# A tuned attention and NF4 feed-forward kernel on one core: the block sums of x for the second token unit made by GpSimd in place of VectorE

## The chip, the cores and the metric

The kernel runs on one core of one Trainium2 chip. The metric is device time in microseconds (us), from one execution to the next of the same program; less is better. A core has five engines that run their own instruction streams and meet only through semaphores: TensorE (PE in the profile) multiplies, VectorE (DVE), ScalarE (ACT) and GpSimd (POOL) work elementwise, and SyncE (SP) issues the DMAs here. SBUF is the on-chip memory, PSUM holds the results of TensorE.

## What is computed

Two layers, each with a residual. The first normalizes each token, lets the 4 sequences attend to each other at each position, and adds. The second normalizes again and runs a gated feed-forward layer whose weights come as 4-bit codes with a scale per block of 64.

```python
x = L0_attn_x                                    # 4 x 512 x 1024
x = x + attn(layernorm(x))                       # per position: softmax(q q^T / sqrt(512)) q, and q added
h = layernorm(x)
g = einsum('bsh,mh->bsm', h, Wg)                 # Wg, Wu: 3584 x 1024, code table[q] * absmax
u = einsum('bsh,mh->bsm', h, Wu)
x = x + einsum('bsm,hm->bsh', silu(g) * u, Wd)   # Wd: 1024 x 3584
```

## The kernel before, in words

**Numbers.** Each float32 operand of the feed-forward products is split in a high and a low float16 half, and a product is three matmuls: high by high, high by low, low by high. Matrices are cut in 2 x 2 blocks, and most products are made with seven block multiplications in place of eight, at the price of sums of blocks. For x these sums are four, T1 to T4, kept in the places XT1, XT4, XT3, XT2 of the block index. They need the float32 blocks, which ScalarE puts there first ("whole"), and `t_sums` turns one quarter of a unit (one of the 4 sequences, index n) from whole blocks into the four sums in a buffer of its own, `t_sum`. Then `t_high` (ScalarE, L691) writes the high halves of the sums over the whole blocks, and `t_low` (VectorE, L1142) writes the low halves.

**Stages.** The tokens are two units (unit 0 in `xa`, unit 1 in `xb`). After attention (to about 104 us) the kernel makes eight plain half products, `half(0)` to `half(7)`, of the first pair of gate and up weight tiles, for unit 0 and then for unit 1; 4 x 12 matmuls each. While they run, the sums of x are prepared. From `p1(PLAIN)` on (slot 4) every slot has the seven products p1, p2, p4, p6, p3, p5, p7 in an order written out by hand. The down projection follows from about 1147 us.

**Who does what around the change.** Every engine's order is written by hand. VectorE: `h_sums(1)`, `scale_codes(4)`, `sum_blocks(4)`, `h_low(1)`, then `t_sums(1, 0)`, `t_sums(1, 1)`, `t_low(1, 0)`, `weight_halves(4)` (a cast, L1038, and a subtraction, L1042), `scale_codes(5)` (L1010), `sum_blocks(5)` (L1017 to L1020), `weight_halves(5)`, `h_of_half(6)` (L1152), `t_sums(1, 2)`, `t_low(1, 1)`, `t_sums(1, 3)`, `h_of_half(7)`, `t_low(1, 2)`, `t_low(1, 3)` and on to slot 4's work. ScalarE: `silu_of_half(4)`, bends of the codes (L641, eight steps for each weight tile half), `t_high(1, 0)`, `silu_of_half(5)`, `t_high(1, 1)`, three bends, `t_high(1, 2)`, three bends, `t_high(1, 3)`, four bends, `s1_copy(PLAIN)` (L711). TensorE waits in `p1(PLAIN)` for the weights of jobs 4 and 5 (`w_done`), in `p2(PLAIN)` for `h_of_half(7)`, and in `p6(PLAIN)` for `s1_copy(PLAIN)`. `p6(PLAIN + 1)` is the first that needs all sums of unit 1.

**Buffers.** `t_sum[unit][n % 2]` is double: the sums of n = 0 and 2 share one buffer, those of 1 and 3 the other. So the sums of n = 2 wait for `t_low` of n = 0, those of 3 for `t_low` of 1. For unit 1 the first buffer overlaps `s_up`, which `h_low(1)` reads last; the second overlaps `ring1`, which a store to DRAM (`h1_out`) has to have read.

**GpSimd** does the last normalizations of x (`normalized(k)`, L606), and its program ends with them at about 139 us.

Of the kernel before, what the change touches and what calls it, by code (L numbers as in the profile page):

```python
# [6 lines left out]
B, C, L = 4, 512, 1024  # L7
M = 3584
BLOCK = 64
CT = C // P  # L10
# [33 lines left out]
X11, X21, XT1, XT4, X22, XT3, XT2 = range(7)  # L44
# [59 lines left out]
def block_kernel(nc: bass.Bass, x, q_stream, a_stream, absmax, out, x1_mem, h_out):  # L104
    F32, F16, I32 = mybir.dt.float32, mybir.dt.float16, mybir.dt.int32
    ALU = mybir.AluOpType
# [4 lines left out]
    with ctx:  # L111
# [3 lines left out]
        def sem(name):  # L115
            return ctx.enter_context(nc.semaphore(name))
# [48 lines left out]
        def absm_at(k):  # L165
# [4 lines left out]
            if k >= DOWN_JOBS - 1:  # L170
# [5 lines left out]
               for t in (xa[:, 8192:12288], xb[:, 8192:12288], rw[:, 4096:8192], rw[:, 0:4096])]  # L176
# [15 lines left out]
        x_whole = [t[:, :].rearrange("p (b n w) -> p b n w", b=7, n=B) for t in (xa, xb)]  # L192
        t_sum = [[t.rearrange("p (b t) -> p b t", b=4) for t in (gs[:, 2048:4096], rw[:, 0:2048])],
                 [t.rearrange("p (b t) -> p b t", b=4) for t in (rw[:, 3584:5632], rw[:, 0:2048])]]
# [40 lines left out]
        x1_out = [sem(f"x1_out{c}") for c in range(CT)]  # L235
        h1_out = sem("h1_out")
# [29 lines left out]
        xn_ready = sem("xn_ready")  # L266
        t2_done = sem("t2_done")
        xact_done = sem("xact_done")
        xlo_done = sem("xlo_done")
        t3_done = sem("t3_done")  # L270
        t2s_done = sem("t2s_done")
        t24_done = sem("t24_done")
        g_half = sem("g_half")
        u_half = sem("u_half")
        silu_half = sem("silu_half")
# [2 lines left out]
        tlo_done = sem("tlo_done")  # L278
# [28 lines left out]
        hlo2_done = sem("hlo2_done")  # L307
# [31 lines left out]
        def pair_blocks(t, n, part):  # L339

            return t[:, 1:7, n, part, :, :].rearrange("p (a b) k t -> p a b (k t)", b=3)[:, :, 1:3, :]
# [35 lines left out]
        def _(sp):  # L377
            def load_codes(k):
                mem, _, t, _ = codes_at(k)
                sp.dma_start(mem, q_stream[k, :, :]).then_inc(codes_in[t], 16)  # L380
# [146 lines left out]
        def _(pool):  # L527
# [76 lines left out]
            def normalized(k):  # L604
                c, n, f = k // 8, k // 2 % B, k % 2
                g.tensor_scalar(xn_buf(k), acc[c][:, n, f * 512:f * 512 + 512],  # L606
                                ln_scale[:, c % 2, n:n + 1], ln_bias[:, c % 2, n:n + 1],
                                ALU.mult, ALU.add).then_inc(xn_ready, 1)
# [16 lines left out]
            for k in range(24, 32):  # L625
                if k % 2 == 0:
                    pool.wait_ge(t2_done, 21 + (k - 24) // 2)
                normalized(k)

        @block.scalar  # L630
        def _(act):
            fn = nc.scalar.activation
# [54 lines left out]
                   ACT.Copy, bias=0.0, scale=1.0).then_inc(xact_done, 1)  # L687

            def t_high(unit, n):
                act.wait_ge(t24_done, B * unit + n + 1)  # L690
                fn(pair_blocks(xt[unit], n, 0), t_sum[unit][n % 2].rearrange("p (a b) t -> p a b t", a=2),  # L691
                   ACT.Copy, bias=0.0, scale=1.0).then_inc(thi_done, 1)

# [110 lines left out]
            bends(4, range(0, 2))  # L804
            silu_of_half(1)
            t_high(0, 0)
            bends(4, range(2, 4))
            t_high(0, 1)
            bends(4, range(4, 6))
            t_high(0, 2)  # L810
            x_blocks(24)
            x_blocks(25)
# [112 lines left out]
        def _(dve):  # L925
# [3 lines left out]
            def link(ins):  # L929
                chained[0] += 1  # L930
                ins.then_inc(v_chain, 1)
                dve.wait_ge(v_chain, chained[0])
# [173 lines left out]
            def x_low(k):  # L1106
                c, n, f = k // 8, k // 2 % B, k % 2
                t, later = c // 2, c % 2
                dve.wait_ge(xact_done, k + 1)
                block = x12[:, n, :, :, :] if later and not f else \  # L1110
                    xt[t][:, (X22 if later else X21 if f else X11), n, :, :, :]
                v.tensor_tensor(block[:, 1, :, :], x_tile(k), block[:, 0, :, :], ALU.subtract).then_inc(xlo_done, 1)

            def t_sums(unit, n):

                m = B * unit + n
                t, whole = t_sum[unit][n % 2], x_whole[unit][:, :, n, :]
                dve.wait_ge(xact_done, 8 * (2 * unit + 1) + 2 * n + 2)
                if n >= 2:
                    dve.wait_ge(tlo_done, m - 1)  # L1120
                elif m == 0:
                    dve.wait_ge(m_done, CT * LG)
                elif m == 1:
                    dve.wait_ge(xn_ready, 2 * CT * B)
                    dve.wait_ge(x1_out[3], 16)
                elif m == B:
                    dve.wait_ge(hlo2_done, 1)
                    dve.wait_ge(xn_ready, 2 * CT * B)
                    dve.wait_ge(x1_out[3], 16)
                elif m == B + 1:  # L1130
                    dve.wait_ge(h1_out, 16)
                v.tensor_tensor(t[:, 2, :], whole[:, XT2, :], whole[:, XT3, :], ALU.subtract).then_inc(t3_done, 1)
                v.tensor_tensor(t[:, 0, :], whole[:, XT3, :], whole[:, XT1, :], ALU.subtract)
                dve.wait_ge(t3_done, m + 1)
                v.tensor_tensor(t[:, 3, :], t[:, 2, :], whole[:, XT1, :], ALU.add).then_inc(t2s_done, 1)
                dve.wait_ge(t2s_done, m + 1)
                v.tensor_tensor(t[:, 1, :], whole[:, XT4, :], t[:, 3, :], ALU.subtract).then_inc(t24_done, 1)

            def t_low(unit, n):
                t = t_sum[unit][n % 2]  # L1140
                dve.wait_ge(thi_done, B * unit + n + 1)
                v.tensor_tensor(pair_blocks(xt[unit], n, 1), t.rearrange("p (a b) t -> p a b t", a=2),  # L1142
                                pair_blocks(xt[unit], n, 0), ALU.subtract).then_inc(tlo_done, 1)
# [90 lines left out]
            def h_low(s):  # L1234
                n, unit = nth(s), slot_at(s)[2]
                dve.wait_ge(hhi1_done, n + 1)
                v.tensor_tensor(ring1[:, :, :, 1, :].rearrange("p n b t -> p b n t"),
                                act_mem[unit].rearrange("p b (n t) -> p b n t", n=B),
                                ring1[:, :, :, 0, :].rearrange("p n b t -> p b n t"), ALU.subtract).then_inc(hlo1_done, 1)
                dve.wait_ge(hhi2_done, n + 1)  # L1240
                v.tensor_tensor(ring2[:, :, :, 1, :].rearrange("p n b t -> p b n t"),
                                s_up.rearrange("p b (n t) -> p b n t", n=B),
                                ring2[:, :, :, 0, :].rearrange("p n b t -> p b n t"), ALU.subtract).then_inc(hlo2_done, 1)
# [46 lines left out]
            weight_low(3)  # L1290
            for k in range(20, 24):
                x_low(k)
            t_sums(0, 0)
            t_sums(0, 1)
            t_low(0, 0)
            t_sums(0, 2)
            t_low(0, 1)
            h_of_half(2)
            x_low(24)
            x_low(25)  # L1300
            t_sums(0, 3)
            x_low(26)
            x_low(27)
            t_low(0, 2)
# [7 lines left out]
            scale_codes(4)  # L1312
            sum_blocks(4)
            h_low(1)
            t_sums(1, 0)
            t_sums(1, 1)
            t_low(1, 0)
            weight_halves(4)
            scale_codes(5)
            sum_blocks(5)  # L1320
            weight_halves(5)
            h_of_half(6)
            t_sums(1, 2)
            t_low(1, 1)
            t_sums(1, 3)
            h_of_half(7)
            t_low(1, 2)
            t_low(1, 3)
# [483 lines left out]
```

## Time and profile before

| | before |
|---|---|
| median of 3 runs (lowest, highest) | 1668.82 us (1667.91, 1668.83) |
| the profiled execution: its time, its span | 1667.4 us, 1665.7 us |
| busy: TensorE, VectorE, ScalarE, GpSimd | 98%, 72%, 62%, 4% |
| mean granted TensorE clock | 0.998 of full speed |

The span runs from the first to the last instruction of the profiled execution; times of single instructions are counted from its start. Busy shares are means over the whole span and say little about a stage. The rows below come from four kinds of view: the chain of work that ended last, the busy time in chosen stretches, the timeline of one engine, and the list of one source line. A bracket at the end of a timeline row is the time that the engine stood idle before the row, and who released it.

### The profile page before, as it was taken

Reading aid. Unit: us, or ns where it says so; the run is one execution under the profiler, and the core shown is the slowest. Engines: PE = TensorE matmul, PEld = TensorE weight load, DVE = VectorE, ACT = ScalarE, POOL = GpSimd, SP = SyncE. Lnnn points to the kernel's source line nnn. Section 1 sums busy time; section 2 is a strip of 40 time slices with the busy share of each in tenths; the row PEclk is TensorE's granted clock in tenths of the full one; section 3 lists DMA queues with packets and bytes.
Section 4 is the critical chain, followed back from the end, with each engine's and each line's share of the span. In section 5 each row is a group of like instructions: output and inputs, shape, how many; then the busy total and the mean of one; then the engine's idle time right before and its main releaser. Section 6 shows DMA issues by size and latency. Waiting matters only on the chain.

```text
span 1665.7 us, 20171 instructions
## 1 busy us (share of the span) xinstructions
PE 1630.1 (98%) x7888; PEld 786.5 (47%) x7888; DVE 1202.4 (72%) x1540; ACT 1030.1 (62%) x1118; POOL 59.8 (4%) x98
## 2 busy tenths in 40 slices
PE   6889999999999999999999999999899999999999
PEld 6865444444444444444444444444344444444444
DVE  7888967685766767576686767678777767577566
ACT  5679676776766667676666767688786526352000
POOL 4261000000000000000000000000000000000000
PEclk9999999999999999999999999999999999999999
DMA  6340232331422233142233314243764444343773
GB/s 269 114 165 14 95 120 95 120 139 52 161 91 104 95 121 139 51 164 95 96 103 112 140 51 165 95 151 100 258 249 176 150 150 175 125 175 126 254 258 123
DMA packets 76895, 226.39 MB, mean 136 GB/s; under 512 B 5248, under 2 KB 19968, under 8 KB 76288
## 3 DMA queue, kind: packets, MB, share of 16 engines
q1 hardware_dynamic: 76800, 225.10, 37.7%
q8 instruction: 62, 1.02, 0.3%
q14 instruction: 33, 0.27, 0.0%
HBM read 156.93 MB, written 68.16 MB: 135 GB/s over the span
## 4 chain that ended last, share of the span: by engine, by line
PE 93%; DVE 3%; ACT 2%; issue 1%; DMA 1%; POOL 0%; SPq 0%; DVEq 0%; POOLq 0%
PE ps L1553 20%; PE ps L1555 20%; PE ps L1554 20%; PE ps L1691 10%; PE ps L1692 10%; PE ps L1693 10%; PE ps L1523 2%; DVE stats L938 1%; PE ps L1532 1%; ACT codes L641 1%; PE ps L1509 0%; DMA codes<-q_dram 0%; DMA xa<-x_dram 0%; ACT xa L691 0%; POOL ln_scale L572 0%
## 5 line engine op out<-in xcount | busy, mean ns | idle before, releaser
L641 ACT ACTIVATE codes<-codes 128x1024 f32<-128x1024 f32 (+1 forms) x672 | 708.1, 1055 | 153.8 <-DMA codes<-q_dram 139.9
L1386 DVE SCALAR_TENSOR_TENSOR xb<-ps,y_back,xb 128x512 f32<-128x512 f32 x140 | 103.9, 749 | 73.5 <-PE ps L1693 68.9
L1553 PE MATMUL ps<-xa,wg 128*128 128x512 f16 x388 | 147.0, 379 | 1.1 <-issue 1.1
L1553 PE MATMUL ps<-xb,rw 128*128 128x512 f16 x388 | 147.1, 379 | 0.7 <-ACT gs L723 0.7
L1553 PE MATMUL ps<-xa,rw 128*128 128x512 f16 x388 | 147.1, 379 | 0.0
L1554 PE MATMUL ps<-xa,rw 128*128 128x512 f16 x388 | 147.1, 379 | 0.0
L1555 PE MATMUL ps<-xa,rw 128*128 128x512 f16 x388 | 147.1, 379 | 0.0
L1553 PE MATMUL ps<-xb,wg 128*128 128x512 f16 x388 | 147.1, 379 | 0.0
L1554 PE MATMUL ps<-xb,wg 128*128 128x512 f16 x388 | 147.1, 379 | 0.0
L1555 PE MATMUL ps<-xb,wg 128*128 128x512 f16 x388 | 147.1, 379 | 0.0
L1554 PE MATMUL ps<-xb,rw 128*128 128x512 f16 x388 | 147.1, 379 | 0.0
L1555 PE MATMUL ps<-xb,rw 128*128 128x512 f16 x388 | 147.1, 379 | 0.0
L1555 PE MATMUL ps<-xa,wg 128*128 128x512 f16 x388 | 147.1, 379 | 0.0
L1554 PE MATMUL ps<-xa,wg 128*128 128x512 f16 x388 | 147.1, 379 | 0.0
L723 ACT ACTIVATE gs<-ps 128x512 f32<-128x512 f32 x52 | 31.0, 596 | 138.6 <-PE ps L1555 138.6
L1386 DVE SCALAR_TENSOR_TENSOR xa<-ps,y_back,xa 128x512 f32<-128x512 f32 x84 | 62.4, 749 | 55.3 <-PE ps L1693 43.7
L1010 DVE SCALAR_TENSOR_TENSOR tmp<-codes,w_scale,absm 128x1024 f32<-128x1024 f32 x69 | 88.2, 1278 | 3.2 <-ACT codes L641 2.9
L1042 DVE TENSOR_TENSOR rw<-tmp,rw 128x1792 f16<-128x1792 f32 (+1 forms) x36 | 71.3, 1981 | 3.5 <-ACT rw L767 2.3
L1205 DVE TENSOR_TENSOR gs<-ps,gs 128x512 f32<-128x512 f32 x26 | 17.9, 688 | 75.5 <-PE ps L1555 75.5
L1691 PE MATMUL ps<-rw,gs 128*128 128x512 f16 x189 | 71.6, 379 | 0.0
L1692 PE MATMUL ps<-rw,gs 128*128 128x512 f16 x189 | 71.6, 379 | 0.0
L1693 PE MATMUL ps<-rw,gs 128*128 128x512 f16 x189 | 71.6, 379 | 0.0
(278 smaller groups left out, 2914.3 us busy)
## 6 DMA issues: line engine op xcount, KB each, us to landing
codes<-q_dram SPq DMA_DIRECT2D x84, 512.0 KB, 4.6
absm<-a_dram SPq DMA_DIRECT2D x69, 512.0 KB, 3.7
h_dram<-rw SPq DMA_DIRECT2D x28, 1024.0 KB, 4.2
gs<-h_dram SPq DMA_DIRECT2D x21, 1344.0 KB, 5.9
h_dram<-rw SPq DMA_DIRECT2D x28, 768.0 KB, 4.6
rw<-h_dram SPq DMA_DIRECT2D x11, 896.0 KB, 5.8
rw<-x_dram SPq DMA_DIRECT2D x16, 512.0 KB, 11.0
xa<-a_dram SPq DMA_DIRECT2D x13, 512.0 KB, 5.4
```

Of the source, the lines that this page charges most:

```text
L641: fn(real, real if step else whole, ACT.Prelu, bias=at0, scale=slope, alpha=left).then_inc(bends_done, 1)
L723: fn(u3_buf, ps[:, s % 2, :], ACT.Copy, bias=0.0, scale=1.0).then_inc(u3_ready, 1)
L1010: v.scalar_tensor_tensor(out=tmp[:, 0:4, :].rearrange("p b t -> p (b t)"), in0=codes_at(k)[1], scalar=w_scale[:, mat:mat + 1], in1=largest ...
L1042: v.tensor_tensor(half_of(k, 1), plain_blocks if k < PLAIN else all_blocks, half_of(k, 0), ALU.subtract).then_inc(w_done, 1)
L1386: return v.scalar_tensor_tensor(out=dst, in0=ps[:, bank, :], scalar=y_back[:, 0:1], in1=dst, op0=ALU.mult, op1=ALU.add)
L1523: last = mm(bank[:, :, b, :], y_t[:, lb, :], d_mat[lb // 16][:, lb % 16, :, :], start=True, stop=True)
L1553: mm(dst, w_hi, x_hi, start=(start and kt == 0), stop=False, skip_group_check=True)
L1554: mm(dst, w_hi, x_lo, start=False, stop=False, skip_group_check=True)
L1555: last = mm(dst, w_lo, x_hi, start=False, stop=(kt == 3), skip_group_check=True)
L1691: mm(ps[:, bank, :], h_hi, w_hi, start=(start and at == 0), stop=False, skip_group_check=True)
L1692: mm(ps[:, bank, :], h_hi, w_lo, start=False, stop=False, skip_group_check=True)
L1693: last = mm(ps[:, bank, :], h_lo, w_hi, start=False, stop=ends, skip_group_check=True)
```

## The change

The four subtractions and additions of `t_sums` for unit 1, for each n, are taken out of VectorE's program and stand at the end of GpSimd's, after the last `normalized(k)`. They wait for the same things as before. After the first and the third, GpSimd waits for its own result before it goes on. A new semaphore, `t24_pool`, tells ScalarE's `t_high` of unit 1 that a row of sums is there. VectorE's order is otherwise the same, with the four calls left out. `t_high` and `t_low` are not changed: the halves stay on ScalarE and VectorE. Unit 0 is not changed.

```diff
--- before.py
+++ after.py
@@ -270,6 +270,7 @@
         t3_done = sem("t3_done")
         t2s_done = sem("t2s_done")
         t24_done = sem("t24_done")
+        t24_pool = sem("t24_pool")
         g_half = sem("g_half")
         u_half = sem("u_half")
         silu_half = sem("silu_half")
@@ -627,6 +628,23 @@
                     pool.wait_ge(t2_done, 21 + (k - 24) // 2)
                 normalized(k)
 
+
+            for n in range(B):
+                t, whole = t_sum[1][n % 2], x_whole[1][:, :, n, :]
+                pool.wait_ge(xact_done, 26 + 2 * n)
+                if n >= 2:
+                    pool.wait_ge(tlo_done, B + n - 1)
+                elif n == 0:
+                    pool.wait_ge(hlo2_done, 1)
+                    pool.wait_ge(x1_out[3], 16)
+                    pool.wait_ge(xn_ready, 2 * CT * B)
+                else:
+                    pool.wait_ge(h1_out, 16)
+                link(g.tensor_tensor(t[:, 2, :], whole[:, XT2, :], whole[:, XT3, :], ALU.subtract))
+                g.tensor_tensor(t[:, 0, :], whole[:, XT3, :], whole[:, XT1, :], ALU.subtract)
+                link(g.tensor_tensor(t[:, 3, :], t[:, 2, :], whole[:, XT1, :], ALU.add))
+                g.tensor_tensor(t[:, 1, :], whole[:, XT4, :], t[:, 3, :], ALU.subtract).then_inc(t24_pool, 1)
+
         @block.scalar
         def _(act):
             fn = nc.scalar.activation
@@ -687,7 +705,7 @@
                    ACT.Copy, bias=0.0, scale=1.0).then_inc(xact_done, 1)
 
             def t_high(unit, n):
-                act.wait_ge(t24_done, B * unit + n + 1)
+                act.wait_ge(t24_pool if unit else t24_done, n + 1)
                 fn(pair_blocks(xt[unit], n, 0), t_sum[unit][n % 2].rearrange("p (a b) t -> p a b t", a=2),
                    ACT.Copy, bias=0.0, scale=1.0).then_inc(thi_done, 1)
 
@@ -1111,29 +1129,22 @@
                     xt[t][:, (X22 if later else X21 if f else X11), n, :, :, :]
                 v.tensor_tensor(block[:, 1, :, :], x_tile(k), block[:, 0, :, :], ALU.subtract).then_inc(xlo_done, 1)
 
-            def t_sums(unit, n):
-
-                m = B * unit + n
-                t, whole = t_sum[unit][n % 2], x_whole[unit][:, :, n, :]
-                dve.wait_ge(xact_done, 8 * (2 * unit + 1) + 2 * n + 2)
+            def t_sums(n):
+
+                t, whole = t_sum[0][n % 2], x_whole[0][:, :, n, :]
+                dve.wait_ge(xact_done, 10 + 2 * n)
                 if n >= 2:
-                    dve.wait_ge(tlo_done, m - 1)
-                elif m == 0:
+                    dve.wait_ge(tlo_done, n - 1)
+                elif n == 0:
                     dve.wait_ge(m_done, CT * LG)
-                elif m == 1:
+                else:
                     dve.wait_ge(xn_ready, 2 * CT * B)
                     dve.wait_ge(x1_out[3], 16)
-                elif m == B:
-                    dve.wait_ge(hlo2_done, 1)
-                    dve.wait_ge(xn_ready, 2 * CT * B)
-                    dve.wait_ge(x1_out[3], 16)
-                elif m == B + 1:
-                    dve.wait_ge(h1_out, 16)
                 v.tensor_tensor(t[:, 2, :], whole[:, XT2, :], whole[:, XT3, :], ALU.subtract).then_inc(t3_done, 1)
                 v.tensor_tensor(t[:, 0, :], whole[:, XT3, :], whole[:, XT1, :], ALU.subtract)
-                dve.wait_ge(t3_done, m + 1)
+                dve.wait_ge(t3_done, n + 1)
                 v.tensor_tensor(t[:, 3, :], t[:, 2, :], whole[:, XT1, :], ALU.add).then_inc(t2s_done, 1)
-                dve.wait_ge(t2s_done, m + 1)
+                dve.wait_ge(t2s_done, n + 1)
                 v.tensor_tensor(t[:, 1, :], whole[:, XT4, :], t[:, 3, :], ALU.subtract).then_inc(t24_done, 1)
 
             def t_low(unit, n):
@@ -1290,15 +1301,15 @@
             weight_low(3)
             for k in range(20, 24):
                 x_low(k)
-            t_sums(0, 0)
-            t_sums(0, 1)
+            t_sums(0)
+            t_sums(1)
             t_low(0, 0)
-            t_sums(0, 2)
+            t_sums(2)
             t_low(0, 1)
             h_of_half(2)
             x_low(24)
             x_low(25)
-            t_sums(0, 3)
+            t_sums(3)
             x_low(26)
             x_low(27)
             t_low(0, 2)
@@ -1312,17 +1323,13 @@
             scale_codes(4)
             sum_blocks(4)
             h_low(1)
-            t_sums(1, 0)
-            t_sums(1, 1)
             t_low(1, 0)
             weight_halves(4)
             scale_codes(5)
             sum_blocks(5)
             weight_halves(5)
             h_of_half(6)
-            t_sums(1, 2)
             t_low(1, 1)
-            t_sums(1, 3)
             h_of_half(7)
             t_low(1, 2)
             t_low(1, 3)
```

## Rows read from the trace of the kernel before

**Rows 1.** The page: the chain that ended last by engine; one DMA group.

```profile
PE 93%; DVE 3%; ACT 2%; issue 1%; DMA 1%; POOL 0%; SPq 0%; DVEq 0%; POOLq 0%
...
codes<-q_dram SPq DMA_DIRECT2D x84, 512.0 KB, 4.6
```

**Rows 2.** Stretches: length, busy us PE, PEld, DVE, ACT, POOL, clock, DMA share, GB/s.

```profile
161.00:216.00 55.00, 55.00 (x257) 24.89 (x255) 51.96 (x58) 40.60 (x39) 0.00 (x0) 1.00 0.26 92
216.00:700.00 484.00, 484.00 (x2244) 219.44 (x2243) 332.40 (x397) 337.82 (x365) 0.00 (x0) 1.00 0.31 109
...
1174.00:1176.00 2.00, 1.84 (x5) 0.74 (x6) 1.59 (x3) 1.97 (x3) 0.00 (x0) 0.52 1.05 399
1176.00:1178.00 2.00, 2.00 (x8) 0.70 (x6) 1.97 (x4) 1.20 (x3) 0.00 (x0) 0.63 0.25 90
```

**Rows 3.** TensorE timeline: start us, duration us, line, out<-in, idle before and releaser.

```profile
207.61 0.38 PE L1553 MATMUL ps<-xa,wg 128*128 128x512 f16 x1
...
1174.16 0.61 PE L1691 MATMUL ps<-xa 128*128 128x512 f16 x1 [4.64 <-ACT xa L884]
...
1231.71 0.39 PE L1691 MATMUL ps<-rw 128*128 128x512 f16 x1 [1.36 <-DVE rw L1042]
```

**Rows 4.** VectorE timeline, 175 to 204 us.

```profile
175.15 0.69 DVE L1132 TENSOR_TENSOR rw<-xb 128x512 f32<-128x512 f32 x1
...
179.65 0.69 DVE L1137 TENSOR_TENSOR rw<-xb,rw 128x512 f32<-128x512 f32 x1
180.26 2.29 DVE L1142 TENSOR_TENSOR xb<-rw,xb 128x2048 f16<-128x2048 f32 x1
...
185.75 1.28 DVE L1010 SCALAR_TENSOR_TENSOR tmp<-codes,w_scale,absm 128x1024 f32<-128x1024 f32 x1
...
189.97 2.03 DVE L1042 TENSOR_TENSOR wg<-tmp,wg 128x1792 f16<-128x1792 f32 x1
192.27 1.28 DVE L1152 SCALAR_TENSOR_TENSOR gs<-ps,u_back,gs 128x1024 f32<-128x1024 f32 x1 [0.27 <-PE ps L1555]
...
196.00 2.29 DVE L1142 TENSOR_TENSOR xb<-rw,xb 128x2048 f16<-128x2048 f32 x1
...
200.32 0.69 DVE L1137 TENSOR_TENSOR rw<-xb,rw 128x512 f32<-128x512 f32 x1
202.63 1.28 DVE L1152 SCALAR_TENSOR_TENSOR gs<-ps,u_back,gs 128x1024 f32<-128x1024 f32 x1 [1.62 <-PE ps L1555]
```

**Rows 5.** ScalarE timeline, 177 to 208 us.

```profile
177.81 1.91 ACT L691 ACTIVATE xb<-rw 128x2048 f16<-128x2048 f32 x1 [0.93 <-DVE rw L1137]
...
201.06 1.90 ACT L691 ACTIVATE xb<-rw 128x2048 f16<-128x2048 f32 x1
...
206.94 0.58 ACT L711 ACTIVATE gs<-ps 128x512 f32<-128x512 f32 x1
```

**Rows 6.** Prices on GpSimd: a source line (ns min/median/max), and timelines around 52.7 us.

```profile
L606 POOL TENSOR_SCALAR xb<-rw,ln_scale,ln_bias x16: 762/768/815, 113.6 to 138.3; 128x512 f32<-128x512 f32 x16
...
52.73 2.95 POOL L595 TENSOR_TENSOR xa<-gs,mask 128x1024 f32<-128x1024 f32 x1 [5.32 <-DVE gs L989]
...
52.69 1.23 DVE L996 TENSOR_TENSOR xa<-gs,mask 128x1024 f32<-128x1024 f32 x1
```

**Rows 7.** GpSimd and VectorE timelines where the two engines meet.

```profile
98.99 0.24 POOL L574 TENSOR_SCALAR ln_scale<-ln_scale 128x4 f32<-128x4 f32 x1
99.31 0.20 POOL L575 TENSOR_TENSOR ln_bias<-mean_var,ln_scale 128x4 f32<-128x4 f32 x1
...
111.82 1.08 POOL L574 TENSOR_SCALAR ln_scale<-ln_scale 128x4 f32<-128x4 f32 x1
...
111.52 1.27 DVE L1010 SCALAR_TENSOR_TENSOR tmp<-codes,w_scale,absm 128x1024 f32<-128x1024 f32 x1
...
137.51 1.52 POOL L606 TENSOR_SCALAR xb<-rw,ln_scale,ln_bias 128x512 f32<-128x512 f32 x2
...
138.65 0.92 DVE L1132 TENSOR_TENSOR gs<-xa 128x512 f32<-128x512 f32 x1
```

## The prediction

> **What bounds the kernel now.** I read the chain of waits first. It is TensorE for 93% of the span, with VectorE, ScalarE and the DMAs sharing the rest [rows 1]. So a change counts only if it moves a TensorE instruction. The table by stretch says where that can happen: from 161 us to 700 us TensorE is busy without a hole (55.00 of 55.00 us, then 484.00 of 484.00 us) at a granted clock of 1.00, the upper level of 2.4 GHz [rows 2]. The sixteen subtractions and additions that the change moves (the `t_sums(1, n)`) lie between 175.15 and 201.01 us [rows 4], inside that stretch. There is no TensorE wait there to win back. Taking load off VectorE brings nothing at that place, although it is busy for 51.96 of the 55 us; what is left to ask is which engine that is early by little becomes late.
>
> The tightest place is found by putting the TensorE timeline beside ScalarE's. The first matmul of `p6(4)` starts at 207.61 us, and it waits for `s1_copy(4)` on ScalarE, which runs from 206.94 for 0.58 us, to 207.52. The slack is 0.09 us [rows 3, 5]. ScalarE gets to that copy without a pause: `t_high(1, 3)` starts at 201.06 and lasts 1.9, four bends follow, and the copy starts 5.88 us after it. And `t_high(1, 3)` waits for the last sum of row 3, which ends on VectorE at 200.32 + 0.69 = 201.01 [rows 4, 5]. So the end of the fourth row of sums sets, almost to the tenth of a microsecond, when TensorE gets on. `p2(4)`, which needs `h_of_half(7)`, follows behind `p1(4)` and has over 1 us: one product of 2.6 us before 207.61, about 205.0, against 202.63 + 1.28 = 203.9 [rows 3, 4].
>
> **The change part by part.**
>
> *Removed from VectorE:* 4 rows of 4 instructions. Two rows take 175.15 to 180.34, 5.1 us until the next instruction starts at 180.26, and rows 2 and 3 about 2.5 us each: some 10 us [rows 4]. Worth nothing by itself, as above.
>
> *Added to GpSimd:* the same 16 instructions, 128x512 float32 with two SBUF inputs, plus two waits for an own result in each row. No such instruction is in the trace. Lower bound: GpSimd's one-input pass over the same shape, 0.768 us. Upper bound: half of its two-input pass over 1024 elements, 2.95/2 = 1.48 us [rows 6]. That second row may hold waiting: VectorE's L996, of two SBUF inputs and 1.23 us, started 0.04 us ahead of it. All of it taken off, 1.72/2 = 0.86. I take the middle of the outer bounds, 1.12 us, since the upper row is of the right kind but perhaps not free of waiting, and the lower is free of it but of the wrong kind. A row is then 4 x 1.12 + 2 x 0.08 = 4.6 us (0.08 is the gap after a waited-for small GpSimd instruction: 98.99 + 0.24 to 99.31) against 2.5 on VectorE. GpSimd has nothing behind these instructions in its own queue, and issues no DMA.
>
> Of the price the Trainium skill has a figure, in "GPSIMD Engine Reference", section 3.1: 4497 ns for a two-input pass over 2048 elements. An estimate from that is 1.12 us for 512, the value that I have from the rows.
>
> *Do the two engines run side by side?* The trace says not always. At 111.82 a GpSimd instruction on 128x4 takes 1.08 us where the same line took 0.24; it ends at 112.90, when VectorE's L1010 (two SBUF inputs, 111.52 + 1.27 = 112.79) has ended. The other way round, VectorE's L1132 starts at 138.65 and takes 0.92 us in place of 0.69, and of its work the larger part, 0.54 us, comes after GpSimd's last L606, which ended at 139.03 [rows 7]. So each has waited until the other's instruction was finished. VectorE instructions with one input in PSUM did not do this: the L606 have 762 to 815 ns through many of them [rows 6]. Nearly all that VectorE has to do between `t_low(1, 0)` and `weight_low(5)` is of two SBUF inputs. I therefore add the two engines' times there instead of overlapping them. Not shown is whether the two take turns in a long row of instructions, and whether the casts (L1038) take part.
>
> The Trainium skill's "SBUF — State Buffer", section "Who interferes with whom", has the same as a rule: a VectorE instruction with two SBUF inputs and a GpSimd instruction that reads SBUF exclude each other for the whole instruction, the later one waits, and the casts can be in it too. But then L996 should have held up the 2.95 us row by its full 1.2 us, and what is left, 0.86 for 512 elements, is not the 1.12 of the other page; both cannot be whole. The sum by 0.86 is a rival below.
>
> *The walk*, with before in brackets:
> 1. Row 0 starts where it did, when `h_low(1)` is done, at 175.15: done 175.15 + 4.6 = 179.8 (`t_high(1, 0)` began at 177.81). VectorE stands at the wait of `t_low(1, 0)`, and `weight_halves(4)`, `scale_codes(5)`, `sum_blocks(5)` and `weight_halves(5)` stand behind it. Where it worked 5.1 us it now idles about 7.
> 2. `t_high(1, 0)` takes 1.91: 181.75. GpSimd is by then in the second instruction of row 1, until 182.1; there `t_low(1, 0)` gets through (180.26).
> 3. VectorE's own work from there to the end of `weight_low(5)` is 180.26 to 192.00, 11.74 us. GpSimd has 6 instructions left of rows 1 and 2, 6.7 us, and they are wedged in between: 182.1 + 11.7 + 6.7 = 200.5 [rows 4, 5]. TensorE wants these weights at `p1(4)`, two products before 207.61. A half product of 48 matmuls lasts 202.63 - 192.27 = 10.36 us, so a product of 12 lasts 2.59, and `p1(4)` starts at 202.4: in time.
> 4. `h_of_half(6)` 1.2, `t_low(1, 1)` 2.2: 203.9 (198.3). Row 3 waits for this `t_low`, since it reuses the buffer of row 1.
> 5. Row 3 is 4.6 us: 208.5. `h_of_half(7)` reads PSUM and runs beside it, to 205.1, but `t_low(1, 2)` then takes its 2.2 us in the middle: 210.7 (201.01).
> 6. `t_high(1, 3)` at 210.8 (201.06), +9.7; ScalarE's four bends and `s1_copy(4)` follow as before; TensorE's `p6(4)` is late by 9.7 - 0.1 = 9.6 us.
>
> If VectorE never lets GpSimd in while it has work, the walk differs: row 1's last two sums wait until about 193.5, `h_of_half(6)` covers the first, `t_high(1, 1)` ends at 197.6 and `t_low(1, 1)` at 200.2; row 2, cut by that `t_low`, ends at 202.5, row 3, cut by `t_low(1, 2)`, at 209.3: +8.2 us. The middle of the two orders is 8.9.
>
> *The clock.* Before a 4.64 us hole of TensorE the clock was granted whole; after it, the matmuls of 1174 to 1178 us ran at 0.52 and 0.63, about the lower level of 1.2 GHz: 2 x 0.48 + 2 x 0.37 = 1.7, less the idle start, 1.6 us lost [rows 2, 3]. A hole of 8 to 9 us at 207 should cost the same: +1.6.
>
> *Queues.* SyncE's `load_after(5)` waits for `scale_codes(5)`, before at 185.75, and fetches the codes that ScalarE bends four steps into the last stretch. Moved by at most 8 us and with 4.6 us to landing [rows 1, 4], these codes come by 199, before 204.9, where they were first used (the last two of the four bends, 1.0 us each, before 206.94) [rows 5]; free. After `p6(4)`, VectorE has `t_low(1, 3)` and the weights of job 6 left, late by no more than TensorE is, and TensorE has five products ahead of the next thing that it takes from VectorE. I price that at nothing; if that cover were gone it would cost up to the 2.2 us of one `t_low`.
>
> Sum: 8.9 + 1.6 = 10.5 us on the profiled execution's 1667.4 us (span 1665.7 and 1.7 around it), which lies 1.4 below the median; on the median, 1668.8 + 10.5 = 1679.3 us. Bounds with the engines excluding each other: at 0.77 us an instruction, row 0 is done at 178.4, `weight_low(5)` at 180.7 + 11.7 + 5 x 0.77 = 196.2, `t_low(1, 1)` at 199.6, row 3 at 202.9: +1.8, and a hole that short did not lower the clock (1.36 at 1231.7) [rows 3]. At 1.48: 184.2 + 11.7 + 8.9 = 204.8, 208.2, 216.5: +15.4 and 1.6, so 1685.8.
>
> **The rivals.** *Cheap sums* (0.86 us, contended): row 0 at 178.7, `weight_low(5)` at 181.3 + 11.7 + 5 x 0.86 = 197.3, `t_low(1, 1)` at 200.7, row 3 at 204.3: +3.2, with the clock +4.8: 1673.6 us. For it: the L996 row. At the 0.77 end it is within 0.2%.
>
> *No contention* (the other side): the engines overlap in truth, the long GpSimd rows of the trace being exceptions. Then row 0 ends at 179.8, `t_low(1, 0)` starts at 181.8, `weight_low(5)` ends at 193.5, `t_low(1, 1)` at 196.9, row 3 at 201.5: +0.4, 1669.2 us. Below about 1.1 us an instruction it gives nothing at all, from there on 8 us for each us; at 1.48 it gives +3.2. Against it: both rows 7.
>
> *Faster.* The freed 10 us would have to reach the two later holes of TensorE, 4.64 and 1.36 us with 1.6 of clock, 7.6 us at most: 1661 us. It needs VectorE to be behind at 1165, while it is not in arrears anywhere after 216 (332.40 busy of 484) [rows 2]; nearly excluded. That the sums do not really move is a rival without a chance: each wait of the diff's `t_high` and `t_low` hangs on GpSimd's own semaphore.
>
> **How the numbers follow.** Contended at the price taken: 0.59, 1679.3 us. Cheap sums: 0.18. No contention: 0.19. Faster: 0.04. The range leaves out some of the ends: 1669.0 takes in no contention, 1684.0 takes in a price of about 1.4 us. A measurement of this kernel can tell 0.2%, 3.3 us, from no change. Slower by more: all of the first case and two thirds of the second, 0.70. Within: 0.26. Faster: 0.04.
>
> **What would show it.** Right: a hole of TensorE at `p6(4)` of some 9 us that ends with `s1_copy(4)`; GpSimd's L-lines of the new sums with spans well over their shortest, and VectorE's L1142, L1042 and L1017 to L1020 in 180 to 200 us longer than before; the second half of `t_sums` row 3 cut by a `t_low`. Wrong: spans of VectorE unchanged there (no exclusion), or a shortest sum under 0.9 us (price), or a full clock after the hole. The prediction fails mainly with the price, since each 0.1 us of it moves the end by about 1.9 us.

## The result and the profile after

The changed kernel takes 1680.69 us (median of 6 runs, 1679.37 to 1682.11) against 1668.82 us (median of 6 runs beside it). The ratio is 1.0073, with a 95% interval of 1.0062 to 1.0083: slower by 11.9 us. The prediction was 1679.3 us, slower.

| | before | after |
|---|---|---|
| median | 1668.82 us | 1680.69 us |
| span of the profiled execution | 1665.7 us | 1677.8 us |
| mean granted TensorE clock | 0.998 | 0.993 |
| GpSimd busy | 59.8 us | 87.8 us |
| first matmul of `p6(4)` | 207.61 us | 217.52 us |

Line numbers after the change are higher: `t_low` is L1153 (was L1142), `t_high` L709 (L691), the cast L1056 (L1038), the weights' subtraction L1060 (L1042), `s1_copy` L729 (L711), `h_of_half` L1163 (L1152), `scale_codes` L1028 (L1010). GpSimd's four sums of a row are L643 to L646.

The list of waits of the changed kernel, from 175 to 225 us (engine and line, who it waited for, total, times, longest), has TensorE in it, which had no wait in this stretch before [rows 2]:

```profile
...
ACT xb L709 <- POOL rw L646: 21.1, 4, 9.6
DVE xb L1153 <- ACT xb L709: 12.9, 2, 7.3
...
PE ps L1560 <- ACT gs L729: 9.8, 1, 9.8
POOL rw L643 <- DVE xb L1153: 7.5, 1, 7.5
```

Read upward from TensorE it is the whole story: `p6(4)` waited 9.8 us for `s1_copy(4)`; ScalarE had waited up to 9.6 us for a row of sums; GpSimd had waited 7.5 us for the `t_low` that frees the buffer of row 3; and VectorE's first `t_low` had waited 7.3 us for the halves of row 0.

GpSimd's timeline of the changed kernel (start, duration, idle before) shows what a sum costs there and where it was held up:

```profile
175.19 1.27 POOL L643 TENSOR_TENSOR rw<-xb 128x512 f32<-128x512 f32 x1 [36.17 <-DVE rw L1252]
176.55 1.26 POOL L644 TENSOR_TENSOR rw<-xb 128x512 f32<-128x512 f32 x1
177.77 1.26 POOL L645 TENSOR_TENSOR rw<-rw,xb 128x512 f32<-128x512 f32 x1
179.11 1.26 POOL L646 TENSOR_TENSOR rw<-xb,rw 128x512 f32<-128x512 f32 x1
...
182.90 3.32 POOL L645 TENSOR_TENSOR rw<-rw,xb 128x512 f32<-128x512 f32 x1
186.29 2.00 POOL L646 TENSOR_TENSOR rw<-xb,rw 128x512 f32<-128x512 f32 x1
188.25 3.06 POOL L643 TENSOR_TENSOR rw<-xb 128x512 f32<-128x512 f32 x1
191.39 2.14 POOL L644 TENSOR_TENSOR rw<-xb 128x512 f32<-128x512 f32 x1
193.48 1.45 POOL L645 TENSOR_TENSOR rw<-rw,xb 128x512 f32<-128x512 f32 x1
195.01 1.33 POOL L646 TENSOR_TENSOR rw<-xb,rw 128x512 f32<-128x512 f32 x1
203.87 1.27 POOL L643 TENSOR_TENSOR rw<-xb 128x512 f32<-128x512 f32 x1 [7.54 <-DVE xb L1153]
205.22 3.19 POOL L644 TENSOR_TENSOR rw<-xb 128x512 f32<-128x512 f32 x1
208.37 1.26 POOL L645 TENSOR_TENSOR rw<-rw,xb 128x512 f32<-128x512 f32 x1
209.71 1.26 POOL L646 TENSOR_TENSOR rw<-xb,rw 128x512 f32<-128x512 f32 x1
```

Alone, a sum takes 1.26 us. Beside VectorE it takes 1.33 to 3.32 us: little more where VectorE's instructions are short (128x256), much more where they are long. VectorE's timeline over the same time has the other half:

```profile
182.34 2.75 DVE L1153 TENSOR_TENSOR xb<-rw,xb 128x2048 f16<-128x2048 f32 x1 [7.29 <-ACT xb L709]
185.01 2.15 DVE L1056 CAST wg<-tmp 128x1792 f16<-128x1792 f32 x1
187.20 2.97 DVE L1060 TENSOR_TENSOR wg<-tmp,wg 128x1792 f16<-128x1792 f32 x1
190.31 2.08 DVE L1028 SCALAR_TENSOR_TENSOR tmp<-codes,w_scale,absm 128x1024 f32<-128x1024 f32 x1
192.42 1.38 DVE L1035 TENSOR_TENSOR tmp<-tmp 128x256 f32<-128x256 f32 x1
193.84 1.37 DVE L1036 TENSOR_TENSOR tmp<-tmp 128x256 f32<-128x256 f32 x1
195.13 1.48 DVE L1037 TENSOR_TENSOR tmp<-tmp 128x256 f32<-128x256 f32 x1
196.65 0.43 DVE L1038 TENSOR_TENSOR tmp<-tmp 128x256 f32<-128x256 f32 x1
...
198.31 2.03 DVE L1060 TENSOR_TENSOR wg<-tmp,wg 128x1792 f16<-128x1792 f32 x1
...
201.45 2.28 DVE L1153 TENSOR_TENSOR xb<-rw,xb 128x2048 f16<-128x2048 f32 x1
```

Before, the same instructions took 2.29, 1.09, 2.03, 1.28 and, four times, 0.43 us. The first, third and fourth are in [rows 4]; the cast and the short ones, from VectorE's timeline of the kernel before:

```profile
182.47 1.09 DVE L1038 CAST wg<-tmp 128x1792 f16<-128x1792 f32 x1
...
187.06 0.43 DVE L1017 TENSOR_TENSOR tmp<-tmp 128x256 f32<-128x256 f32 x1
187.52 0.43 DVE L1018 TENSOR_TENSOR tmp<-tmp 128x256 f32<-128x256 f32 x1
```

Seven in a row are longer, by 0.46, 1.06, 0.94, 0.80, 0.95, 0.94 and 1.05 us, 6.2 us in all; the eighth, once GpSimd is through with row 2, is as short as ever. Between two long ones stands one GpSimd sum each time: the engines took turns, strictly.

ScalarE's timeline ends the chain. `t_high(1, 3)` starts at 211.00, 9.94 us after its 201.06 of before [rows 5]:

```profile
211.00 1.91 ACT L709 ACTIVATE xb<-rw 128x2048 f16<-128x2048 f32 x1 [9.59 <-POOL rw L646]
212.82 4.16 ACT L659 ACTIVATE codes<-codes 128x1024 f32<-128x1024 f32 x4
216.89 0.58 ACT L729 ACTIVATE gs<-ps 128x512 f32<-128x512 f32 x1
```

And TensorE's, around the hole and at its end:

```profile
207.38 0.38 PE L1562 MATMUL ps<-xa,wg 128*128 128x512 f16 x1
217.52 0.61 PE L1560 MATMUL ps<-xa,wg 128*128 128x512 f16 x1 [9.76 <-ACT gs L729]
217.92 0.63 PE L1561 MATMUL ps<-xa,wg 128*128 128x512 f16 x1
...
220.48 0.55 PE L1561 MATMUL ps<-xa,wg 128*128 128x512 f16 x1
220.87 0.38 PE L1562 MATMUL ps<-xa,wg 128*128 128x512 f16 x1
```

Eight matmuls are spaced 0.43 us instead of 0.22. The ninth start after the first, 221.09, is 3.57 us behind 217.52, where nine spacings of 0.216 make 1.94: 1.6 us lost to the clock. So the 12.1 us of span are 9.9 us late at `p6(4)`, 1.6 us of half clock behind it, and 0.6 us at the old hole of the down projection, where TensorE restarts at 1185.66 instead of 1174.16 (11.5 later, the first two terms) and has 11 slow matmuls instead of 8, 0.21 us each.

### The profile page after: what moved, and what is told of

It reads as the page before. It is cut to its first block, busy times and chain, and to the rows that moved or that the text cites. A ratio compares the mean times of both kernels' runs of the same rounds, so it can differ in the third digit from the quotient of the medians.

```text
span 1677.8 us, 20171 instructions
## 1 busy us (share of the span) xinstructions
PE 1633.8 (97%) x7888; PEld 787.4 (47%) x7888; DVE 1198.8 (71%) x1524; ACT 1030.3 (61%) x1118; POOL 87.8 (5%) x114
## 4 chain that ended last, share of the span: by engine, by line
PE 90%; DVE 5%; ACT 2%; issue 1%; POOL 1%; DMA 1%; POOLq 0%; SPq 0%; DVEq 0%
PE ps L1560 19%; PE ps L1561 19%; PE ps L1562 19%; PE ps L1698 10%; PE ps L1699 10%; PE ps L1700 10%; PE ps L1530 2%; DVE stats L956 1%; PE ps L1516 1%; PE ps L1539 1%; ACT codes L659 1%; DMA codes<-q_dram 0%; ACT xa L709 0%; DVE tmp L1028 0%; POOL rw L644 0%
## 5 line engine op out<-in xcount | busy, mean ns | idle before, releaser
L1028 DVE SCALAR_TENSOR_TENSOR tmp<-codes,w_scale,absm 128x1024 f32<-128x1024 f32 x69 | 89.0, 1290 | 3.2 <-ACT codes L659 2.9
L1060 DVE TENSOR_TENSOR rw<-tmp,rw 128x1792 f16<-128x1792 f32 (+1 forms) x36 | 71.3, 1981 | 3.5 <-ACT rw L785 2.3
```

The source lines that it names most:

```text
L1028: v.scalar_tensor_tensor(out=tmp[:, 0:4, :].rearrange("p b t -> p (b t)"), in0=codes_at(k)[1], scalar=w_scale[:, mat:mat + 1], in1=largest ...
L1060: v.tensor_tensor(half_of(k, 1), plain_blocks if k < PLAIN else all_blocks, half_of(k, 0), ALU.subtract).then_inc(w_done, 1)
```

## The experiments

All are compared with the kernel before on the same chip. The whole stretch starts up to 1.8 us later or 0.9 us earlier than in the kernel before, for reasons that lie ahead of the change: TensorE's wait for VectorE near 49 us is 2.4 to 4.4 us long, the eight matmuls behind it take 1.10 us in some traces and 1.97 us in others, and the clock behind a 2.45 us wait near 121 us differs (last section). In the changed kernel's trace these differences cancel: the sums start at 175.19, before at 175.15. So TensorE's waits and the distances between instructions are compared here, not the absolute times. "Slow matmuls" are those behind the hole that take over 0.5 us; at full clock they take 0.38. Waits and slow matmuls are read from one execution of each kernel, medians and ratios from all of them.

| kernel | TensorE's waits in 195 to 225 us | slow matmuls | median, us | ratio (95%) |
|---|---|---|---|---|
| changed | 9.76 | 8 | 1680.69 | 1.0073 (1.0062 to 1.0083) |
| sums replaced by a write-only fill | 0.83 | 0 | 1669.35 | 1.0006 (0.9997 to 1.0014) |
| the same, longer | 2.33 | 0 | 1672.39 | 1.0023 (1.0014 to 1.0032) |
| half of each sum | none | 0 | 1668.31 | 0.9997 (0.9987 to 1.0006) |
| only row 2 on GpSimd | 0.5 | 0 | 1669.29 | 1.0006 (0.9996 to 1.0016) |
| only row 3 on GpSimd | 2.41 | 0 | 1671.90 | 1.0020 (1.0011 to 1.0029) |
| rows 2, 3 on GpSimd | 3.14 | 7 | 1674.08 | 1.0033 (1.0021 to 1.0045) |
| rows 0, 1 on GpSimd | 1.30, 2.54 | 8 | 1675.39 | 1.0033 (1.0021 to 1.0046) |
| third buffer | 1.89, 0.56, 0.28 | 0 | 1671.78 | 1.0018 (1.0009 to 1.0028) |
| before, with ScalarE delayed | 10.71 | 9 | 1682.54 | 1.0085 (1.0071 to 1.0099) |
| changed, `p5(4)` first | 7.16, 0.69 | 12 | 1678.62 | 1.0059 (1.0044 to 1.0074) |

### Does reading exclude, or only length?

```diff
-                link(g.tensor_tensor(t[:, 2, :], whole[:, XT2, :], whole[:, XT3, :], ALU.subtract))
-                g.tensor_tensor(t[:, 0, :], whole[:, XT3, :], whole[:, XT1, :], ALU.subtract)
-                link(g.tensor_tensor(t[:, 3, :], t[:, 2, :], whole[:, XT1, :], ALU.add))
-                g.tensor_tensor(t[:, 1, :], whole[:, XT4, :], t[:, 3, :], ALU.subtract).then_inc(t24_pool, 1)
+                flat = t.rearrange("p b t -> p (b t)")[:, 0:1232]
+                for _ in range(3):
+                    link(g.memset(flat, 100.0))
+                g.memset(flat, 100.0).then_inc(t24_pool, 1)
```

> Left out: the sums themselves. GpSimd fills the rows of sums of unit 1 with a constant, 1232 elements for each of the 16 instructions, so that each should take about as long (1.25 us) but reads no SBUF; all waits stay, and each row has one more wait for an own result. Theory (the engines exclude each other because both read SBUF): row 0 ends at 180.4, no VectorE instruction is longer than before, weight_low(5) ends near 194.1, row 3 near 202.8, and p6(4) is late by 1.8 us (209.4): 1670.6 us, +0.1%. Rival (only the length of the GpSimd instructions matters, or any two instructions exclude each other): as the changed kernel, p6(4) near 217.5, 1680 us.

The fill took 1.12 us, not 1.25, and a row 4.6 us. TensorE waited 0.83 us, not 1.8, as rows 0 and 3 were each some 0.5 us shorter than meant. Of VectorE's instructions one alone was longer, and it is the one that is not a two-input instruction. VectorE's and GpSimd's timelines of this kernel where they meet:

```profile
185.01 1.38 DVE L1056 CAST wg<-tmp 128x1792 f16<-128x1792 f32 x1
186.42 2.03 DVE L1060 TENSOR_TENSOR wg<-tmp,wg 128x1792 f16<-128x1792 f32 x1
...
184.32 1.12 POOL L646 MEMSET rw<- 128x1232 f32 x1
185.38 4.43 POOL L645 MEMSET rw<- 128x1232 f32 x3
```

L1060 has its old 2.03 us with a fill running beside it; it had 2.97 beside a sum. The cast has 1.38 in place of 1.09, since the fill of 184.32 ran until 185.44, and the three fills behind take 4.43 us, where the other rows' three take 3.49: they waited for the cast. So, in these two kernels, a two-input VectorE instruction excludes a GpSimd instruction that reads, and not one that only writes; the cast excludes both.

The Trainium skill has this in "SBUF — State Buffer", section "Who interferes with whom": a VectorE instruction with two SBUF inputs contends with a GpSimd instruction that reads SBUF and not with one that only writes, while one in a two-port mode, which a cast can enter, contends with GpSimd either way. These rows agree with it, and so do the seven long instructions of the changed kernel.

The fill was shorter than meant, so the test was repeated with 1384 elements:

```diff
-                flat = t.rearrange("p b t -> p (b t)")[:, 0:1232]
+                flat = t.rearrange("p b t -> p (b t)")[:, 0:1384]
```

> As the write-only kernel before it, the sums left out, but with 1384 elements an instruction, so that a row lasts as long as a row of real sums (5.1 us; it was 4.6). Theory (what reading costs on top of length is the exclusion): rows 0 and 3 each 0.5 us longer, p6(4) late by 0.8 + 1.0 = 1.8 us, full clock, +0.1%: 1670.5 us. Rival (the write-only kernel was fast because its rows were short): p6(4) late by over 4 us.

A row took 5.12 us, as long as a row of real sums. TensorE waited 2.33 us at full clock in the profiled execution (1669.64 us), 0.5 us more than expected: the cast now took 1.88 us, 0.8 more than alone. Nine of the eleven executions took 1671.6 to 1673.4, at a mean clock of 0.995 to 0.996 in place of 0.997. The likely reading is that the clock fell in those, since 2.3 us of hole and 1.6 us of clock make the 3.9 us by which the median is longer; but no trace shows one of them. The expected 1670.5 us left this out. Of the 9.8 us of the hole, then, length makes 2.3 (the cast's waiting in it), and what comes on top comes with reading.

### Is it the length of a sum, or the handover?

```diff
+                t, whole = t[:, :, 0:256], whole[:, :, 0:256]
```

> Left out: half of the sums. Each of GpSimd's 16 instructions takes 256 of the 512 columns of its blocks, everything else as in the changed kernel. Theory (the price is the length of the two-input pass, about 0.65 us for half): weight_low(5) near 195.2, row 3 done near 201.5, p6(4) late by 0.5 us and no fall of the clock: 1669.3 us. Rival (a fixed cost of the handover to GpSimd, its semaphores and its start, carries it): still over +4 us.

A sum of 256 columns took 0.73 us (median of L644: 731 ns), and the hole was gone; `s1_copy(4)` was in time, where I had expected it 0.5 us late. All semaphores, waits and positions are those of the changed kernel, so the handover by itself costs nothing that counts. From 0.73 us for 256 and 1.26 for 512 follow 2.07 ns for each element and 0.20 us fixed.

### Which rows cost it?

Four kernels put some rows back on VectorE, at their old places and with their old waits. Each has this edit with its own tuple, and the calls of `t_sums` for the other rows:

```diff
+POOL_ROWS = (2, 3)
...
-            for n in range(B):
+            for n in POOL_ROWS:
...
```

Rows 0 and 1 back:

> Rows 0 and 1 of the sums of unit 1 go back to VectorE, rows 2 and 3 stay on GpSimd. Theory: t_low(1, 0) starts at 180.26 as before; row 2's four sums (1.26 us each) are wedged into VectorE's 11.7 us, weight_low(5) at 197.0, t_low(1, 1) until 200.5, row 3 until 207.9 with one t_low in the middle; p6(4) late by 6.9 us, plus 1.6 us of clock: +8.4 us, 1677.2. Rival (each moved row costs the same): half of the changed kernel, +6 us. Rival (row 0's late start is what counts): below +3 us.

TensorE waited 3.14 us, not 6.9. Two steps were off. Row 2 lengthened four VectorE instructions by 0.95, 0.80, 0.94 and 0.94 us, 3.6 us in all, where I had charged 4 x 1.26. And no `t_low` cut row 3: VectorE's and GpSimd's timelines of this kernel:

```profile
204.42 1.28 DVE L1176 SCALAR_TENSOR_TENSOR gs<-ps,u_back,gs 128x1024 f32<-128x1024 f32 x1 [3.60 <-PE ps L1577]
205.62 4.87 DVE L1166 TENSOR_TENSOR xb<-rw,xb 128x2048 f16<-128x2048 f32 x2
...
203.53 1.27 POOL L648 TENSOR_TENSOR rw<-rw,xb 128x512 f32<-128x512 f32 x1
204.88 1.27 POOL L649 TENSOR_TENSOR rw<-xb,rw 128x512 f32<-128x512 f32 x1
```

`h_of_half(7)` (L1176 here) had to wait for TensorE, and `t_low(1, 2)` behind it came when the last sum already ran; `t_low` waited 0.4 us for it, and no sum waited 2 us for a `t_low`. The rival "half the price for half the rows" gave +6, closer to the measured +5.5 than my +8.4, but the next runs show that the rows do not share the price evenly.

> Only row 2 of the sums of unit 1 on GpSimd, rows 0, 1 and 3 on VectorE. Theory: four sums wedged into VectorE's stretch, weight_low(5) at 197.0 in place of 192.0, t_low(1, 1) until 200.5, row 3 by VectorE until 203.0: p6(4) late by 2.0 us, no fall of the clock, 1670.8. Rival (no exclusion counts here, VectorE is freed of 2.5 us): p6(4) on time.

> Only row 3 of the sums of unit 1 on GpSimd. VectorE has nothing of two SBUF inputs to do beside it. Theory: t_low(1, 1) ends at 198.3, row 3 takes 5.15 in place of 2.6 us, until 203.5, t_high(1, 3) at 203.6 in place of 201.06: p6(4) late by 2.4 us, no fall of the clock, 1671.2. Rival (moved work is hidden, ScalarE has slack): p6(4) on time.

Row 2 alone: 0.5 us of wait, for the same reason (3.6 us of lengthening, not 5.0), and 1.0006, which can't be told from no change. Row 3 alone: 2.41 us where 2.4 was expected, from nothing but the longer row (5.2 against 2.6 us), as no two-input instruction of VectorE ran beside it; every GpSimd sum there took 1.26 or 1.27 us. It is the row with the least slack behind it. The clock was full behind this hole in the profiled execution, 1671.19 us; the others went up to 1674.22 us, at mean clocks down to 0.994 against 0.996, so it may have fallen in some of them.

> Rows 0 and 1 of the sums of unit 1 on GpSimd, rows 2 and 3 back on VectorE. Theory: as the changed kernel until t_low(1, 0) at 182.3; only the last two sums of row 1 are wedged in, some 2.2 us, weight_low(5) near 196.2; then VectorE's own rows, t_low(1, 1) until 202.1, row 3 until 204.7: p6(4) late by 3.7 us and the clock falls as it did after 3.14 us: +5.2 us, 1673.9. Rival (the moved rows 0 and 1 come ahead of the tight part and cost nothing): p6(4) on time.

Rows 0 and 1: the last three sums of row 1 lengthened VectorE's `t_low`, cast and subtraction by 2.5 us. With `t_low(1, 0)` late by 2.1, `h_of_half(7)`, now behind the two rows of VectorE, came too late for `p2(4)` (1.30 us), and `s1_copy(4)` for `p6(4)` (2.54): 3.84 together, 3.7 expected. Two executions took 1672.6 and 1673.0 us and three 1675.4 to 1675.7, so the median says little here; the ratio makes +5.5 us, 5.2 expected. The first rows are not covered although 25 us of other work lie behind them, because VectorE has hardly a pause in between (0.27 us before `h_of_half(6)` in the kernel before, and 1.62 only before `h_of_half(7)` [rows 4]).

### Is the buffer of row 3 the link?

```diff
-                 [t.rearrange("p (b t) -> p b t", b=4) for t in (rw[:, 3584:5632], rw[:, 0:2048])]]
+                 [t.rearrange("p (b t) -> p b t", b=4) for t in (rw[:, 3584:5632], rw[:, 0:2048], gs[:, 0:2048])]]
...
-                if n >= 2:
-                    pool.wait_ge(tlo_done, B + n - 1)
+                if n == 3:
+                    pool.wait_ge(tlo_done, B + 1)
+                elif n == 2:
+                    pool.wait_ge(hlo1_done, 1)
...
```

> The changed kernel with a third buffer for the sums of unit 1, in gs[0:2048], which is idle from 173.4 to 211 us: row 2 no longer waits for t_low(1, 0), row 3 waits for t_low(1, 0) in place of t_low(1, 1). Theory: row 3 is done near 204, so the hole at p6(4) goes; but ten GpSimd sums in place of six are wedged into VectorE's stretch, weight_low(5) ends near 205.5, and p1(4) waits for h_of_half(6), 4.3 us, and p2(4) 0.8 more for h_of_half(7); with the clock +6.5 us, 1675.3. Rival (the wait of row 3 for its buffer is not the link): unchanged, +12 us. Rival (the buffer is all that costs): under +1.5 us.

TensorE's timeline of this kernel has the large hole replaced by three small ones. The first two are the waits for `h_of_half(6)` and `h_of_half(7)` that were expected; the third, at `p6(4)`, was to be gone:

```profile
204.88 0.38 PE L1562 MATMUL ps<-xa,wg 128*128 128x512 f16 x1 [1.89 <-DVE gs L1165]
208.19 0.39 PE L1562 MATMUL ps<-xa,wg 128*128 128x512 f16 x1 [0.56 <-DVE gs L1165]
211.23 0.39 PE L1562 MATMUL ps<-xa,wg 128*128 128x512 f16 x1 [0.28 <-ACT gs L731]
```

They add to 2.7 us where I expected 5.1 and a fall of the clock; again the size was that of a wedged sum, 0.9 instead of 1.2 us. The ratio is 1.0018, a quarter of the loss of the changed kernel. It computes the same as the changed kernel and is the better way to have these sums on GpSimd; it does not reach the kernel before.

### Is one late copy the whole price?

```diff
+        pad = sem("pad")
...
             bends(7, range(0, 2))
+            act.wait_ge(hlo1_done, 1)
+            for i in range(10):
+                fn(gs[:, 1024:2048], gs[:, 1024:2048], ACT.Copy, bias=0.0, scale=1.0).then_inc(pad, 1)
+                act.wait_ge(pad, i + 1)
             s1_copy(PLAIN)
```

> The kernel before, all sums on VectorE, with ten chained copies of 128x1024 on ScalarE (1.04 us each) ahead of s1_copy(4). Theory (the slack there is 0.1 us, and the whole price of the change is this one late copy and the clock after it): p6(4) late by 10.3 us, first matmuls at half the clock, +1.6: 1680.7 us, +11.9. Rival (GpSimd's share lies elsewhere too, or the slack is larger): p6(4) late by less than 9 us, or the total smaller than the hole plus 1 us.

In this kernel GpSimd has nothing to do with it. The ten copies took 10.85 us, TensorE waited 10.71 us at the same matmul, and 9 matmuls behind were slow (the changed kernel: 9.76 us, 8). So ScalarE's slack there is 0.1 us, as read from the rows. The total, +13.9 us, is 2.0 above the 11.9 expected. The hole makes 0.4 of that (copies of 1.09 instead of 1.04 us), the clock behind it another 0.4 (2.0 instead of 1.6, from the distance between this hole and the later one), and the clock behind the later hole 0.7 (11 slow matmuls in place of 8); the rest, 0.5 us, lies within the interval of this ratio.

### Can another product fill the hole?

```diff
             p2(PLAIN)
-            p6(PLAIN)
             p5(PLAIN)
+            p6(PLAIN)
```

> The changed kernel with p5(4) ahead of p6(4) on TensorE; p5(4) needs nothing that is late. Theory: p6(4) starts at 217.5 as before it, the hole is 7.2 us, the clock still falls (1.6), and since nothing is left between p6(4) and p7(4), p7(4) now waits 0.8 us for u2_copy(4), until 222.6: 1.7 us earlier than in the changed kernel, 1679.0. Rival (the hole moves whole with p6, no product can fill it): the same as the changed kernel. Rival (the full 2.6 us come back): 1678.1.

The hole was 7.16 us, 2.6 less, and TensorE then stood 0.69 us in front of `p7(4)` for `u2_copy(4)`, both as expected (7.2 and 0.8); the median is 1678.62 against 1679.0. The product fits into the hole, but more matmuls were slow behind it, 12 in place of 8. The median alone can't tell the theory from its two rivals (1680.7 and 1678.1), as the ratio's interval is 2.5 us to either side; the two waits do.

## Why the prediction was right

The walk against the changed kernel's trace, in us:

| step | predicted | measured |
|---|---|---|
| row 0 ends | 179.8 | 180.4 |
| `t_low(1, 0)` gets through | 182.1 | 182.3 to 182.8 |
| `weight_low(5)` ends | 200.5 | 200.3 |
| `t_low(1, 1)` ends | 203.9 | 203.7 |
| row 3 ends, one `t_low` in its middle | 210.7 | 211.0 |
| `p6(4)` late by | 9.6 (alternating), 8.9 (middle of two orders) | 9.9 |
| clock behind the hole | 1.6 | 1.6 |
| in the span | 10.5 | 12.1 |

- *What bounds the kernel, and where it is tight.* Right. The slack of 0.1 us at `s1_copy(4)` was the lever: delaying that copy without GpSimd gave the same hole.
- *Load taken off VectorE brings nothing.* Right. TensorE was full there, and no experiment was clear of no change on the faster side; half of each sum, which takes the same sixteen instructions off VectorE and makes no hole, gave 0.9997.
- *Price of a sum: 1.12 us.* Too low; 1.26. The two rows that bounded it were far apart (0.77 and 1.48). With 2.07 ns an element and 0.20 fixed, the 1024 elements of L595 [rows 6] would take 2.3 us alone, if that instruction, which multiplies by a mask, has the same price. Its 2.95 us then held some 0.6 us of waiting for L996, not the 1.2 that a whole exclusion would have made, for which no run here has a reason; reading the row as half free of waiting was about right, and the middle of the bounds by luck near.
- *The price of the page.* The Trainium skill, "GPSIMD Engine Reference", section 3.1, has 4497 ns for 2048 elements. The runs agree with it: 2.07 ns an element and 0.20 us fixed would make 4.4 us, an estimate. Scaled to 512 elements without a fixed part, 2.2 ns each, it gave 1.12 us and was 0.14 short.
- *The engines exclude each other.* Right, in both directions, and the part that had been left open was shown: they take turns after every instruction, and the cast takes part. So the order behind the 8.2 us, in which VectorE never lets GpSimd in, is out, and mixing it in made the hole 0.7 us too small.
- *How much a wedged sum costs VectorE.* Off: I charged 1.12 us for each of 6. Measured are 0.80 to 1.06 for a sum of 1.26 us, and 0.46 for the first, which was already running. A price too low and a share too high cancelled in the sum here, which was luck: the same walk with 1.26 us has `weight_low(5)` end at 202.2, not 200.5, and the hole at 11.9 us, 2.0 more than measured. They did not cancel in three experiments, worked out with 1.26, which overrated the wedging by 0.3 us a sum.
- *The clock.* Right in kind and size at the new hole. Not foreseen: 0.6 us at the hole that was there before, 11 slow matmuls in place of 8. With the hole itself 1.0 us longer than the 8.9 forecast, that is the 1.6 us between the forecast 10.5 and the 12.1 of the span.
- *Queues.* Right: SyncE's late codes and VectorE's late weights showed in no wait.

## What to carry to other kernels

Before moving elementwise work to GpSimd, list what VectorE runs meanwhile: while its instructions have two SBUF inputs, a GpSimd instruction that reads SBUF doesn't run beside them but between them, so the move adds time to VectorE's queue in place of taking it off. Look for the consumer with the least slack behind each moved piece, not for the engine with the highest load: here the slack was 0.1 us, and a row that is twice as long passed its whole difference on. Where work has moved all the same, another buffer that lets the slow engine start early can give back most of the loss, here three quarters of it.

## What the runs showed of the hardware that was not expected

- Two engines that exclude each other alternate instruction by instruction even where both have a queue without pauses: seven VectorE instructions in a row, of 256 to 2048 elements, each waited for one GpSimd sum. A short instruction suffers most: 0.43 us became 1.38.
- The granted clock after a hole of 2 to 3 us went both ways, and for one and the same hole. All twelve traces have a wait of TensorE of 2.44 or 2.45 us near 121 us, ahead of everything that the change touches. In nine of them, that of the kernel before among them, the clock stayed whole behind it (1.00 from 118 to 130 us). In three (the changed kernel, rows 2 and 3 on GpSimd, the third buffer) it fell after five or six matmuls at full clock, and the same 12 us have 0.86. TensorE's timeline of the changed kernel:

```profile
120.49 0.39 PE L1560 MATMUL ps<-gs,wg 128*128 128x512 f16 x1 [2.45 <-DVE xa L1130]
...
121.58 0.38 PE L1562 MATMUL ps<-gs,wg 128*128 128x512 f16 x1
121.79 0.58 PE L1560 MATMUL ps<-gs,wg 128*128 128x512 f16 x1
```

- In the stretch of the change the same is seen. After 2.41 us the clock was whole, the first matmul behind taking 0.39 us. After waits of 1.30 and 2.54 us, 2.8 us of matmuls between them, it was whole for two matmuls and then half for eight. TensorE's timeline of the kernel with rows 0 and 1 on GpSimd:

```profile
207.62 0.39 PE L1575 MATMUL ps<-xa,wg 128*128 128x512 f16 x1 [1.30 <-DVE gs L1176]
...
212.93 0.39 PE L1575 MATMUL ps<-xa,wg 128*128 128x512 f16 x1 [2.54 <-ACT gs L735]
213.15 0.38 PE L1576 MATMUL ps<-xa,wg 128*128 128x512 f16 x1
213.37 0.57 PE L1577 MATMUL ps<-xa,wg 128*128 128x512 f16 x1
213.73 0.63 PE L1575 MATMUL ps<-xa,wg 128*128 128x512 f16 x1
```

- The hole of 4.6 to 4.9 us in the down projection, the same in all kernels, was followed by 7 to 13 slow matmuls, 0.21 us each. So a difference of about 1 us between single executions of two kernels with such a hole can be the clock alone.
